# Six PSUM banks divided anew in an attention kernel: four for the row maxima, two for the scores

## What is computed

```python
def _mha(x, w_in, b_in, w_out, b_out):       # 16 heads of 16 features
    qkv = x @ w_in.T + b_in
    q, k, v = jnp.split(qkv, 3, axis=-1)     # then split into heads
    scores = jnp.einsum('bhqd,bhkd->bhqk', q, k) / jnp.sqrt(jnp.asarray(hd, x.dtype))
    attn = jax.nn.softmax(scores, axis=-1)
    out = jnp.einsum('bhqk,bhkd->bhqd', attn, v)
    return out @ w_out.T + b_out
for lvl in range(LEVELS):
    x = query[:, ::2 ** lvl, :]
    outs.append(_mha(x, in_proj_w[lvl], in_proj_b[lvl], out_w[lvl], out_b[lvl]))
```

## Time and profile before

| | |
|---|---|
| median of three runs | 4509.1 us (4502.14 to 4513.02) |
| the profiled execution | 4499.3 us, span 4497.5 us |
| TensorE busy | 3904.6 us, 87% |
| VectorE busy | 2645.5 us, 59% |
| ScalarE busy | 2458.9 us, 55% |
| GpSimd busy | 1166.2 us, 26% |
| mean granted TensorE clock | 0.947 of 2.4 GHz |

### The profile page before, as it was taken

The page is one execution under the profiler, slowest core; times in us unless marked ns, Lnnn a source line. Parts: engine busy times, 40 slices in busy tenths (PEclk is TensorE's granted clock), DMA queues, the critical chain, the costliest instruction groups (busy, mean ns, idle before and its releaser), DMA issues. The chain is left out here.

```text
span 4497.5 us, 69641 instructions
## 1 busy us (share of the span) xinstructions
PE 3904.6 (87%) x20881; PEld 2133.0 (47%) x20881; DVE 2645.5 (59%) x4841; ACT 2458.9 (55%) x3163; POOL 1166.2 (26%) x1000
## 2 busy tenths in 40 slices
PE   1789989988988988988998998971999999999998
PEld 1333333333333333333333333321887878778787
DVE  0467777777777777768777777746333333333333
ACT  1366757756756766666675675653444444434443
POOL 3333434433433433343343443120000000000000
PEclk8699999999999999999999999985999999999999
DMA  5343244244344333334424334215000000000000
GB/s 180 83 79 85 83 83 104 83 90 81 101 89 81 99 80 84 90 88 91 94 80 96 82 89 81 43 41 220 9 12 11 18 12 11 12 19 10 11 20 10
DMA packets 308837, 307.37 MB, mean 68 GB/s; under 512 B 75168, under 2 KB 285280, under 8 KB 308192
## 3 DMA queue, kind: packets, MB, share of 16 engines
q1 hardware_dynamic: 299200, 293.59, 27.1%
q10 hardware_dynamic: 9216, 8.39, 0.5%
HBM read 202.28 MB, written 96.47 MB: 66 GB/s over the span
## 5 line engine op out<-in xcount | busy, mean ns | idle before, releaser
L732 ACT ACTIVATE a_probs<-a_p_s 128x1024 f32<-128x1024 f32 x1360 | 1330.0, 1022 | 720.5 <-PE a_p_s L988 677.7
L806 DVE TENSOR_REDUCE a_part_max<-a_p_m 128x1 f32<-128x512 f32 x2048 | 1335.6, 679 | 445.4 <-PE a_p_m L1003 443.0
L1003 PE MATMUL a_p_m<-a_k_st,a_q_st 96*128 96x512 bf16 (+2 forms) x2944 | 1018.9, 381 | 128.6 <-DVE a_part_max L806 68.4
L988 PE MATMUL a_p_s<-a_q_st,a_k_st 98*128 98x512 bf16 (+2 forms) x2944 | 831.8, 371 | 71.5 <-ACT a_probs L732 70.3
L1383 PE MATMUL p_h<-f_h_hi,f_w_hi 128*128 128x512 f32 x2048 | 806.4, 394 | 22.2 <-issue 22.2
L1383 PE MATMUL p_h<-f_h_lo,f_w_hi 128*128 128x512 f32 x2048 | 802.7, 392 | 11.5 <-issue 11.5
L1003 PEld LDWEIGHTS a_p_m<-a_k_st,a_q_st 96*128 96x128 bf16 x2944 | 265.1, 99 | 1037.8 <-DVE a_part_max L806 685.4
L1020 PE MATMUL a_p_o<-a_probs,a_v_aug 128*17 128x512 f32 (+2 forms) x5888 | 745.8, 587 | 0.6 <-ACT a_probs L732 0.6
L1352 DVE TENSOR_TENSOR f_h_lo<-f_h_f,f_h_hi 128x512 fp32r<-128x512 f32 x256 | 177.2, 692 | 707.0 <-ACT f_h_hi L1265 707.0
L806 DVE TENSOR_REDUCE a_row_max<-a_p_m 128x1 f32<-128x512 f32 (+2 forms) x672 | 441.1, 680 | 250.3 <-PE a_p_m L1003 243.6
L1263 ACT ACTIVATE f_h_f<-p_h,f_sc 128x512 f32<-128x512 f32 x256 | 176.6, 690 | 569.2 <-PE p_h L1383 569.1
(11 more groups left out here) (113 smaller groups left out, 4536.0 us busy)
## 6 DMA issues: line engine op xcount, KB each, us to landing
qk_scratch<-a_qk_bf SPq DMA_DIRECT2D x96, 384.0 KB, 2.5
a_w_lo<-wqkv_inner SPq DMA_DIRECT2D x32, 768.0 KB, 4.9
a_q_st<-qk_scratch SPq DMA_DIRECT2D x192, 128.0 KB, 6.7
a_k_st<-qk_scratch SPq DMA_DIRECT2D x192, 128.0 KB, 6.9
a_q_st<-qk_scratch SPq DMA_DIRECT2D x336, 64.0 KB, 2.7
a_k_st<-qk_scratch SPq DMA_DIRECT2D x336, 64.0 KB, 2.7
a_a_lo<-a_attn SPq DMA_DIRECT2D x384, 32.0 KB, 2.0
a_o_lo<-wo_inner SPq DMA_DIRECT2D x24, 512.0 KB, 3.8
```

What stands on the lines that cost most here:

```text
L732: act.activation(probs[:, s % 2, 2 * p:2 * p + 2, :], p_s[:, 2 * p:2 * p + 2, :], ACT.Exp, scale=HD ** -0.5).then_inc(exp_done.sem, 1)
L806: dve.reduce_max(out, src, AX.X).then_inc(max_read.sem, 1)
L988: ins = pe.matmul(p_s[:, j, i * size:(i + 1) * size], k_st[0:ROWS + 2, unit.halves[half], j, key:key + 128], q_st[0:ROWS + 2, unit.place, ...
L1003: ins = pe.matmul(p_m[:, n % 2, r * size:(r + 1) * size], q_st[0:ROWS, unit.place, j, q * 128:(q + 1) * 128], k_st[0:ROWS, unit.halves[kb] ...
```

## The change

The maxima get four banks, the scores two. A max task is now two products into two neighbouring banks, reduced by one VectorE instruction over 1024 columns; there are two such tasks a step. At level 0 the 1024 columns are a whole row of keys, so `part_max`, the maximum of halves and the signal `max_done` go, and the transposes wait for `max_read`. A score task is one bank, with an exponential of its own over 512 columns: four a step, at .2, .25, .6 and .65. The value product of the last step moves from 2.1 to 1.1.

```diff
-MAX_AT = [4 * unit.start for unit in UNITS]
-MAX_OF = [(u, m) for u, unit in enumerate(UNITS) for m in range(4 * unit.tiles)]
+MAX_AT = [2 * unit.start for unit in UNITS]
+MAX_OF = [(u, m) for u, unit in enumerate(UNITS) for m in range(2 * unit.tiles)]
...
-    for m in range(4 * STEPS):
-        p.append((m // 4 - LEAD + (0, .05, .3, .6)[m % 4], "max", m))
+    for m in range(2 * STEPS):
+        p.append((m // 2 - LEAD + (0, .4)[m % 2], "max", m))
...
-        p += [(s + .4, "score", 2 * s), (s + .7, "score", 2 * s + 1), (s + 2.1, "value", s)]
+        p += [(s + (.2, .25, .6, .65)[j], "score", HG * s + j) for j in range(HG)] + [(s + (2.1 if s < STEPS - 1 else 1.1), "value", s)]
...
-        p_s = pb("p_s", [128, 4, 512])
-        p_m = pb("p_m", [128, 2, 512])
+        p_s = pb("p_s", [128, 2, 512])
+        p_m = pb("p_m", [128, 4, 512])
...
-                            score_mm.wait(sp, it, 2 * freed_at(us))
+                            score_mm.wait(sp, it, HG * freed_at(us))
...
-                            s, p = divmod(n, 2)
+                            s, j = divmod(n, HG)
                             act.wait_ge(score_mm.sem, score_mm.value(it, n + 1))
                             value_mm.wait(act, it, s - 1 if s else 0)
-                            act.activation(probs[:, s % 2, 2 * p:2 * p + 2, :], p_s[:, 2 * p:2 * p + 2, :], ACT.Exp,
-                                           scale=HD ** -0.5).then_inc(exp_done.sem, 1)
+                            act.activation(probs[:, s % 2, j, :], p_s[:, j % 2, :], ACT.Exp, scale=HD ** -0.5).then_inc(exp_done.sem, 1)
...
-                            dve.reduce_max(out, src, AX.X).then_inc(max_read.sem, 1)
-                            if lvl == 0 and m == 4 * UNITS[u].tiles - 1:
-                                dve.wait_ge(max_read.sem, max_read.value(it, n + 1))
-                                dve.tensor_tensor(out=slot, in0=part_max[:, u % RING, :, 0], in1=part_max[:, u % RING, :, 1], op=ALU.max)\
-                                   .then_inc(max_done.sem, 1)
+                            outs = 2 * parts // len(UNITS[u].halves)
+                            src = p_m[:, n % 2 * 2:n % 2 * 2 + 2, :].rearrange("p b t -> p (b t)").rearrange("p (r t) -> p r t", r=outs)
+                            dve.reduce_max(slot[:, m * outs:(m + 1) * outs], src, AX.X).then_inc(max_read.sem, 1)
...
                             exp_done.wait(pe, it, n - 1)
-                            for j in (2 * p, 2 * p + 1):
-                                for i in range(parts):
-                                    half, key = divmod(i * size + kt * 128, W)
-                                    ins = pe.matmul(p_s[:, j, i * size:(i + 1) * size], k_st[0:ROWS + 2, unit.halves[half], j, key:key + 128],
+                            for i in range(parts):
+                                half, key = divmod(i * size + kt * 128, W)
+                                ins = pe.matmul(p_s[:, j % 2, i * size:(i + 1) * size], k_st[0:ROWS + 2, unit.halves[half], j, key:key + 128],
...
-                            pe.wait_ge(exp_done.sem, exp_done.value(it, 2 * n + 2))
+                            pe.wait_ge(exp_done.sem, exp_done.value(it, HG * n + HG))
```

More of the change, by code:

```diff
@@ L360, in attention @@
         probs = sb("probs", [128, 2, HG, W])
-        part_max = sb("part_max", [128, RING, NQ * HG, 2])
         row_max = sb("row_max", [128, RING, NQ, HG])
@@ L402, in attention @@
         v_mm, v_done = sig("v_mm", len(V_PAIRS)), sig("v_done", len(V_PAIRS))
-        max_mm, max_read, max_done = sig("max_mm", 4 * STEPS), sig("max_read", 4 * STEPS), sig("max_done", NU - FIRST_FINE)
+        max_mm, max_read = sig("max_mm", 2 * STEPS), sig("max_read", 2 * STEPS)
         neg_mm, neg_read, neg_hi, neg_b = sig("neg_mm", NU), sig("neg_read", NU), sig("neg_hi", NU), sig("neg_b", NU)
         neg_placed = [sig(f"neg_placed{i}", (NU + 1 - i) // 2, 32) for i in range(2)]
-        score_mm, exp_done = sig("score_mm", 2 * STEPS), sig("exp_done", 2 * STEPS)
+        score_mm, exp_done = sig("score_mm", HG * STEPS), sig("exp_done", HG * STEPS)
         value_mm, raw_done = sig("value_mm", STEPS), sig("raw_done", NU)
@@ L800, in steps @@
                             slot = row_max[:, u % RING, :, :].rearrange("p q h -> p (q h)")
-                            if lvl == 0:
-                                out = part_max[:, u % RING, m // 2, m % 2:m % 2 + 1]
-                            else:
-                                out = slot[:, m * parts:(m + 1) * parts]
-                            src = p_m[:, n % 2, :].rearrange("p (r t) -> p r t", r=parts) if parts > 1 else p_m[:, n % 2, :]
-                            dve.reduce_max(out, src, AX.X).then_inc(max_read.sem, 1)
-                            if lvl == 0 and m == 4 * UNITS[u].tiles - 1:
-                                dve.wait_ge(max_read.sem, max_read.value(it, n + 1))
-                                dve.tensor_tensor(out=slot, in0=part_max[:, u % RING, :, 0], in1=part_max[:, u % RING, :, 1], op=ALU.max)\
-                                   .then_inc(max_done.sem, 1)
+                            outs = 2 * parts // len(UNITS[u].halves)
+                            src = p_m[:, n % 2 * 2:n % 2 * 2 + 2, :].rearrange("p b t -> p (b t)").rearrange("p (r t) -> p r t", r=outs)
+                            dve.reduce_max(slot[:, m * outs:(m + 1) * outs], src, AX.X).then_inc(max_read.sem, 1)
                         elif kind == "v":
@@ L926, in steps @@
                         elif kind == "neg":
-                            if n < FIRST_FINE:
-                                max_read.wait(pe, it, MAX_AT[n + 1])
-                            else:
-                                max_done.wait(pe, it, n - FIRST_FINE + 1)
+                            max_read.wait(pe, it, MAX_AT[n + 1] if n + 1 < NU else 2 * STEPS)
                             for q in range(NQ):
@@ L981, in steps @@
                             size = W // parts
-                            if kt == 0 and p == 0:
+                            if kt == 0 and j == 0:
                                 neg_placed[u % 2].wait(pe, it, u // 2 + 1)
                             exp_done.wait(pe, it, n - 1)
-                            for j in (2 * p, 2 * p + 1):
-                                for i in range(parts):
-                                    half, key = divmod(i * size + kt * 128, W)
-                                    ins = pe.matmul(p_s[:, j, i * size:(i + 1) * size], k_st[0:ROWS + 2, unit.halves[half], j, key:key + 128],
-                                                    q_st[0:ROWS + 2, unit.place, j, i * size:(i + 1) * size], start=True, stop=True)
+                            for i in range(parts):
+                                half, key = divmod(i * size + kt * 128, W)
+                                ins = pe.matmul(p_s[:, j % 2, i * size:(i + 1) * size], k_st[0:ROWS + 2, unit.halves[half], j, key:key + 128],
+                                                q_st[0:ROWS + 2, unit.place, j, i * size:(i + 1) * size], start=True, stop=True)
                             ins.then_inc(score_mm.sem, 1)
@@ L998, in steps @@
                             max_read.wait(pe, it, n - 1)
-                            for r in range(parts):
-                                head, kb = divmod(m * parts + r, blocks)
-                                q, j = divmod(head, HG)
-                                key = q * 128 // size * size if parts > 1 else 0
-                                ins = pe.matmul(p_m[:, n % 2, r * size:(r + 1) * size], q_st[0:ROWS, unit.place, j, q * 128:(q + 1) * 128],
-                                                k_st[0:ROWS, unit.halves[kb], j, key:key + size], start=True, stop=True)
+                            for b in range(2):
+                                for r in range(parts):
+                                    head, kb = divmod((2 * m + b) * parts + r, blocks)
+                                    q, j = divmod(head, HG)
+                                    key = q * 128 // size * size if parts > 1 else 0
+                                    ins = pe.matmul(p_m[:, n % 2 * 2 + b, r * size:(r + 1) * size], q_st[0:ROWS, unit.place, j, q * 128:(q + 1) * 128],
+                                                    k_st[0:ROWS, unit.halves[kb], j, key:key + size], start=True, stop=True)
                             ins.then_inc(max_mm.sem, 1)
```

## The result

The changed kernel takes 4622.89 us, median of four runs (4618.3 to 4624.32), against 4511.06 us (4502.14 to 4518.4) before: ratio 1.0247, 95% interval 1.0227 to 1.0267. It is slower, and inside the range, but by 112 us where 210 were forecast. The profiled executions stand at 4499.3 and 4622.9 us, 123.6 apart, since that of before lies 12 us under its median.

A forecast was written before the change was run, and what follows sets the result against it. TensorE in attention, with waits for VectorE's maxima, was taken to bound the kernel. 25.7 us a batch, 205 for eight, plus 5 for late exponentials made 210 on a 4509.1 us median: 4719 us, range 4600 to 4860.

The forecast's parts named there:

- The round trip: TensorE to ScalarE and back inside every step: S2 1.14 us after S0, S2 and S3 waiting 0.53 us together.
- Side steps: Attention steps with a projection or other side product, 35 a batch: 4.24 us becomes 4.77, with nothing to give back.
- late work of ScalarE: Exponentials delayed by ScalarE's weight cast, a dozen a batch, stop TensorE: 0 to 48 us, taken as 5.
- The rival of a general lateness: A third of ScalarE's other work reaches TensorE throughout attention: 180 us on top, 4899 us; chance 0.13.
- Steps with transposes: Attention steps holding transposes of the row maxima, 15 a batch: 3.98 us becomes 4.31, +0.33 each.
- Plain steps: Attention steps without side product or transposes, 35 a batch: 3.13 or 3.41 us becomes 3.38, +0.06 by their counts.
- The stop of about a us: At a batch's last value product, moved one step up: the stop may go, 8 us at most.
- The combination that goes: VectorE's maximum of two half maxima in transposes steps: its removal was taken as already counted in their 3.98 us.
- The lower bound of the exponentials: ScalarE's 512-column exponential at least 511 ns: pair 0.98 us, wait 0.42 us a step, total 62 us lower.
- The maxima's waits: TensorE's maximum matmuls waiting for VectorE: all taken as gone, since VectorE has over a us of slack.
- The clock: the rival: TensorE's clock falls to 1.2 GHz in a quarter of the steps: 320 us more, 5040 us; chance 0.07.

The follow-up runs named there:

- B: Place, not a run: VectorE's combination of half maxima held under GpSimd's weight cut, seven times; with a one-input combination the kernel before takes 4479.16 us.
- A: Place, not a run: the turn between batches, seven times; with only the last value product one step earlier, the kernel before takes 4491.14 us.
- C: Place, not a run: four plain steps a batch of 4.12 us before, three with layer norm work on VectorE, one with four transposes; 3.39 after.

## Why the prediction was right, and where it was not

The direction and its mechanism were right; the size, 210 us for 112, was not.

- **The round trip: right, and shown.** 0.49 + 0.60 + 0.05 gave 1.14 us from S0 to S2; the trace has 1.16, and half an exponential shortened the step by the 0.42 us that two shorter exponentials give. The wait of a step was forecast as 0.53 and is 0.55.
- **Side steps: right, by two errors that cancel.** 4.77 forecast, 4.77 to 4.92 for most of them in the trace. There are 257 and not 280, since the last batch has few, and they grew by 0.57 us each and not 0.53: 148 us for 149. The 0.04 over may be what late work of ScalarE costs, for which the sum had 5 us; that was not tried apart. The rival of a general lateness, with 180 us, did not come.
- **Steps with transposes: the new ones right, the old ones not.** 4.31 forecast and 4.30 in the trace. They are VectorE's, as the run with narrow maxima shows by its 46 us and the one with half an exponential by leaving them at 4.30. But 3.98 for the old ones left out the held ones, of 6.65 and 7.48: their sum grew by 2 us and not by 40, and B is 20 of the difference (the rest of B stands in the plain steps behind them).
- **Plain steps: the other term that failed.** "A plain step [...] +0.25 against 3.13, -0.03 against 3.41, +0.06 by their counts" holds for the regular ones, from a count in 800 us. By those counts (18 of 3.13, 39 of about 3.42) the 300 of the trace would be 998 us; they are 1082. What stood in the other 84 us, steps of A, B and C among it, was what the change could give back, and it gave back half: -24 us for +17.
- **Two sentences named the places and priced them wrongly.** "The stop of about a us that this place has now may go (8 us at most)" was counted at nothing; moving the last value product alone shortens the turns by 29 us and the kernel by 21. "The combination that goes is in the 3.98 already" is true of a combination of 0.175 us and not of the one held 2.84 us: without the hold the kernel before gains 33 us. The second could be seen in the rows of before, as the largest wait behind a short one: 3.2 us in the earlier trace rows, beside a mean of 81.2/64 = 1.3.
- **The range held with some luck.** 4622.89 is 23 us above its lower end. That end was drawn for a shorter exponential and shorter latencies, and neither came; what came had no price. The lower bound of the exponentials was also mis-added: by the working's own rule the pair is 2 x 0.511 - 0.10 = 0.92 us, not 0.98, and the bound 0.37 us a step, not 0.42. With an exponential of 0.597 us nothing hangs on it.
- **The maxima's waits.** "I take every M wait as gone" was right: all waits of maximum matmuls for VectorE now sum to 3.5 us, and those of their weight loads to 14.6. What VectorE cost in the steps of C went with it. That C is VectorE's is shown by half maxima, which shorten it; its share of the change (20 us) was read from the traces and not tried apart.
- **The clock: the rival fell.** Two waits of 0.27 us a step leave the granted clock at 1.00 (rows below), and over attention the clock went up, with fewer stops of several us in it.

The stretch of two steps, profile after, columns as in the earlier trace rows:

```profile
1163.91:1168.73 4.82, 4.60 (x29) 2.26 (x28) 2.45 (x2) 4.10 (x7) 3.82 (x5) 1.00 0.01 3
1492.07:1495.46 3.39, 3.17 (x18) 0.82 (x17) 2.45 (x2) 2.87 (x6) 2.00 (x2) 1.00 0.00 0
```

The Trainium skill ("TensorE: Matmul & The Clock Gate", section on the second failure mode) tells of a kernel cycling through PSUM banks whose micro-idles made the clock oscillate. These stretches don't show that: with two waits a step their granted clock is 1.00.

## What to carry to other kernels

When an engine has two buffers with another engine, price the round trip (hand over, one instruction of the other engine, hand back; here 0.49 + 0.60 + 0.05 us) and ask whether the work between two uses of the same buffer is longer: 0.87 us was not, and cost 3.8%; 1.3 us was, and the same buffers then gave a kernel 3.4% faster than before (1.2% of it is A and B, which the kernel before can have too). Price a kind of step by its whole sum in the trace, not by its commonest length times its count: the difference between the two is what a change may give back. Don't take one batch for all: here the one counted was at the top for two of the three places, and times eight instead of seven they came out a third too large. And look at the longest of a wait or a record beside its mean.

## What the hardware showed that I had not expected

- A VectorE instruction with two SBUF inputs is held to the end of a GpSimd instruction on SBUF that is under way: 2.84 and 1.79 us for one of 0.175, ending with GpSimd's each time; the same work with one SBUF input takes 0.19 us under the same GpSimd instruction. Where it starts first it isn't held: with narrow maxima the combination of 1483.10 takes 0.18 us, and a GpSimd instruction starts 0.02 us behind it.
- Widths: a maximum takes 414, 679 and 1218 ns for 256, 512 and 1024 columns, so 1.04 to 1.05 ns a column and 140 to 150 fixed; the exponential 383, 597 and 1022 ns, so 0.83 and 170. The fixed part that a narrow exponential adds was no surprise; that a wide maximum saves hardly a tenth of a pair was less than its size suggests.
- Short waits of TensorE hardly show in the rows of matmul waits: 0.55 us in each of some 550 steps, about 300 us, appear there as 19 us more.
